# Distance attention: scores in 32x64 parts, weighted values in 128x32 parts, one element deeper

## What is computed

```python
x = x + _L0_xattn_ref(_layernorm(x), ctx, ctx, W_q, W_k, W_v, W_o, query_pos, key_pos, mask)
# in it, b = 32 elements, 16 heads:
scores = jnp.einsum('bhqd,bhkd->bhqk', Q, K) * scale
dist = (query_pos[:, :, None] - key_pos[:, None, :]).astype(scores.dtype)
scores = scores + -_slopes(NUM_HEADS)[None, :, None, None] * dist[:, None, :, :]
scores = jnp.where(mask[:, None, :, :] == 0, -jnp.inf, scores)
m = jnp.max(scores, axis=-1, keepdims=True)
e = jnp.exp(scores - m)
attn = e / (1.0 + jnp.sum(e, axis=-1, keepdims=True))
out = jnp.einsum('bhqk,bhkd->bhqd', attn, V)       # then @ W_o.T
```

## Time and profile before

| | us |
|---|---|
| median of 3 runs (753.58 to 753.89) | 753.7 |
| span of the profiled execution | 751.1 |
| PE busy in it | 662.8 |
| DVE busy | 485.5 |
| ACT busy | 365.0 |
| POOL busy | 310.1 |

### The profile page before, as it was taken

One profiled execution on the slowest core, in us unless ns is written; L12 is line 12 of the kernel. 1 busy time (PEld: TensorE's weight loads), 2 busy tenths in 40 slices (PEclk: granted clock), 3 DMA queues, 4 the chain that ended last, 5 costly groups with the idle time before them and its releaser, 6 DMA issues.

```text
span 751.1 us, 16917 instructions
## 1 busy us (share of the span) xinstructions
PE 662.8 (88%) x6115; PEld 500.4 (67%) x6115; DVE 485.5 (65%) x1367; ACT 365.0 (49%) x992; POOL 310.1 (41%) x458
## 2 busy tenths in 40 slices
PE   4899999999999989985994799988999776999990
PEld 3677878787777778753443586667877673777760
DVE  2686777677768669885488873558888875333330
ACT  1454545545555479874395653436566431222320
POOL 1235455646453179850000031136556513556541
PEclk9999999999999999996997699999999986999995
DMA  8723222322220000019200434538001022243434
GB/s 265 245 62 79 64 78 65 78 65 75 68 72 14 1 3 4 3 44 332 103 0 1 156 125 177 217 125 367 2 3 65 3 99 53 47 69 58 68 40 70
DMA packets 31697, 65.08 MB, mean 87 GB/s; under 512 B 5792, under 2 KB 21792, under 8 KB 29312
## 3 DMA queue, kind: packets, MB, share of 16 engines
q1 hardware_dynamic: 26016, 55.73, 22.8%
q0 software_dynamic: 4688, 7.18, 6.0%
q10 hardware_dynamic: 912, 1.10, 0.5%
HBM read 57.67 MB, written 7.37 MB: 87 GB/s over the span
## 4 chain that ended last, share of the span: by engine, by line
PE 64%; DVE 21%; ACT 5%; issue 4%; DMA 2%; SPq 2%; POOL 1%; DVEq 0%; ACTq 0%; POOLq 0%
PE psum L2627 7%; PE psum L474 6%; PE psum L482 6%; PE psum L496 5%; PE psum L2637 4%; PE psum L521 4%; PE psum L507 4%; PE psum L1482 3%; PE psum L1459 3%; PE psum L837 2%; DVE ff_peak L1500 2%; PE psum L846 2%; PE psum L829 2%; PE psum L877 2%; DMA wn<-in_w_down 2%
## 5 line engine op out<-in xcount | busy, mean ns | idle before, releaser
L415 ACT ACTIVATE prob<-s_sb,negm 128x257 f32<-128x257 f32 x128 | 66.2, 517 | 94.5 <-DVE negm L640 94.5
L782 POOL TENSOR_SCALAR bias<-dist,cst 128x257 f32<-128x257 f32 x128 | 59.8, 486 | 99.5 <-DVE dist L627 89.6
L636 DVE CUSTOM_DVE_ANT_0 s_sb<-psum,bias 128x257 f32<-128x257 f32 x128 | 49.4, 423 | 51.7 <-PE psum L496 48.4
L474 PE MATMUL psum<-ctxT,shared 128*128 128x257 f32 x256 | 62.6, 388 | 2.7 <-DMA msk<-in_mask 2.7
L482 PE MATMUL psum<-shared,ctxT 128*128 128x256 f32 x256 | 60.4, 379 | 0.0
L2627 PE MATMUL psum<-ex_w,shared 128*128 x184 | 58.3, 460 | 0.6 <-ACT shared L2520 0.6
L1721 POOL TENSOR_TENSOR wn<-wn,cst 128x1 f32<-128x1 f32 x8 | 4.7, 589 | 120.4 <-DVE wn L1848 120.4
L474 PEld LDWEIGHTS psum<-ctxT,shared 128*128 128x128 f32 x256 | 47.2, 195 | 9.0 <-issue 3.4
L482 PEld LDWEIGHTS psum<-shared,ctxT 128*128 128x128 f32 x256 | 48.4, 189 | 6.8
L496 PE MATMUL psum<-kT,qbd 64*128 64x257 f32 x256 | 48.4, 429 | 3.0 <-DVE mx L636 2.9
L2627 PEld LDWEIGHTS psum<-ex_w,shared 128*128 128x128 f32 x184 | 33.1, 190 | 15.4 <-issue 0.8
(11 more groups left out here) (359 smaller groups left out, 1655.9 us busy)
## 6 DMA issues: line engine op xcount, KB each, us to landing
ctxT<-in_ctx_T SPq DMA_DIRECT2D x32, 257.0 KB
ex_w<-in_w SPq DMA_DIRECT2D x1, 5632.0 KB, 17.5
kpos<-in_kpos SPq DMA_DIRECT2D x32, 128.5 KB
msk<-in_mask SPq DMA_DIRECT2D x32, 128.5 KB
near_turned<-in_ctx_T_tiles SPq DMA_DIRECT2D x4, 1028.0 KB
ff_used_up<-in_ctx_T_tiles SPq DMA_DIRECT2D x4, 1028.0 KB
near_rows<-in_ctx_tiles SPq DMA_DIRECT2D x4, 1024.0 KB, 8.0
ff_used_up<-in_ctx_tiles SPq DMA_DIRECT2D x4, 1024.0 KB, 7.3
```

What stands on the lines that cost most here:

```text
L415: nc.scalar.activation(prob[n % 2][:, g, :], s_sb[n % 2][:, g, :], ACT.Exp, bias=negm[:, b, g:g + 1], accum_out=esum[t % 2][:, b, g:g + 1]) \
L474: ins = nc.tensor.matmul(kv[m][:, 0:SK], w["xa_k"][:, k, P * m:P * m + P], ctxT[n % BT][:, k, :], start=(k == 0), stop=(k == KT - 1))
L636: nc.vector.tensor_tensor_reduce(s_sb[n % 2][:, g, :], sc[g % 2][:, 0:SK], bias[n % 2][:, g, :], 1.0, float("-inf"), ALU.add, ALU.max, mx[ ...
L782: nc.gpsimd.tensor_scalar(bias[n % 2][:, g, :], dist[n % 2][:], c.slope[:, g:g + 1], 1.0, ALU.mult, ALU.mult).then_inc(bias_ready, 1)
```

## The change

- Scores: eight matmuls of 32x64 parts per element in place of four of 64x128. Row part g takes 32 features, column part m has 64 outputs, each of the four groups has a bank of its own. qbd has two heads where it had four. The banks of the turned probabilities are now two of the scores' banks.
- Which heads belong together changes: the constants for slopes and selection (sel, two, two_quarter) follow.
- Weighted values: 16 matmuls of 128x32 parts with 64 columns in place of 8 of 128x64 with 128 columns; a whole tile of results fits into bank oo, and own_heads_of picks once per tile, in two steps.
- spread(t): the same work in 128x32 parts.
- Distances: two VectorE operations in place of three, with the factor FAR in the slopes taken out again in the bias.
- The lists of all engines are put in a new order: TensorE issues scores(n), weighted(n-2), keys(n+1), turn_p(n-1), values(n+1); VectorE and ScalarE lists follow.

```diff
-        qbd = [sb(f"qbd{i}", [P, KT, BT, 4, SQ]) for i in range(2)]
-        sc, pt, kv, oo, misc = bank[0:2], bank[2:4], bank[4:6], bank[6], bank[7]
+        qbd = [sb(f"qbd{i}", [P, KT, BT, 2, SQ]) for i in range(2)]
+        sc, pt, kv, oo, misc = bank[0:4], bank[0:2], bank[4:6], bank[6], bank[7]
...
+        def turned_at(t):
+            return BT * t + (2 if t == 0 else 0)
...
+            for n in range(N + 1):
+                t = n // BT
                 exps(n - 1, 2)
+                exps(n - 1, 3)
+                if n + 1 < N:
+                    keys(n + 1, 0)
+                    keys(n + 1, 1)
+                if n >= N - 1:
+                    ratio.act(act, n - N - 2)
+                if t + 1 < NT and n == turned_at(t):
                     xT_copy(t + 1)
+                exps(n, 0)
+                if n >= 1:
+                    copy_turned(n - 1)
+                exps(n, 1)
+                if n + 1 < N:
+                    values(n + 1)
...
+            def scores(n):
                 t, b = n // BT, n % BT
+                pe.wait_ge(k_done[0], n + 1)
+                pe.wait_ge(k_done[1], n + 1)
+                pe.wait_ge(qbd_ready, t + 1)
+                at_least(pe, s_done, 4 * n)
+                at_least(pe, pt_done[0], n - 1)
+                at_least(pe, pt_done[1], n - 1)
+                for g in range(NG):
+                    rows = slice(SQ * g, SQ * g + SQ)
+                    for m in range(KT):
+                        ins = nc.tensor.matmul(sc[g][64 * m:64 * m + 64, 0:SK],
+                                               qbd[t % 2][rows, m, b, :, :].rearrange("p h q -> p (h q)"),
+                                               kT[n % 2][rows, m, :], start=True, stop=True)
+                    ins.then_inc(s_full, 1)
 
             def turn_p(n):
                 for j in range(2):
                     pe.wait_ge(p_ready, 4 * n + 2 * j + 2)
                     at_least(pe, pt_done[j], n)
+                    if n + 1 < N:
+                        pe.wait_ge(s_done, 4 * (n + 1) + j + 1)
...
-                if n % 2 == 0:
-                    at_least(pe, keys_read, n // 2)
-                for gp in range(KT):
+                if n % BT == 0:
+                    at_least(pe, keys_read, n // BT)
+                for m in range(KT):
+                    at = P * (n % BT) + 64 * m
                     for i in range(2):
-                        for half in range(2):
-                            g, at = 2 * gp + half, D * (n % 2) + P * gp
-                            ins = nc.tensor.matmul(oo[64 * half:64 * half + 64, at:at + P],
-                                                   v[n % BT][:, i, 64 * g:64 * g + 64], pT[n % 2][:, g, i, :],
-                                                   start=(n % 2 == 0 and gp == 0 and i == 0), stop=True,
+                        for g in range(NG):
+                            own = slice(SQ * g, SQ * g + SQ)
+                            ins = nc.tensor.matmul(oo[own, at:at + 64],
+                                                   v[n % BT][:, i, P * m + SQ * g:P * m + SQ * g + SQ],
+                                                   pT[n % 2][:, g, i, 64 * m:64 * m + 64],
+                                                   start=(n % BT == 0 and m == 0 and i == 0), stop=True,
...
+            for n in range(N + 2):
                 t, b = n // BT, n % BT
                 if n < N:
+                    scores(n)
+                if n >= 2:
                     weighted(n - 2)
                 if b == 2 and t > 0:
                     spread(t - 1)
+                if n + 1 < N:
+                    pe.wait_ge(ctx_loaded[(n + 1) % BT], 48 * ((n + 1) // BT + 1))
+                    keys(n + 1, 0)
+                    keys(n + 1, 1)
+                if t + 1 < NT and n == turned_at(t):
+                    turn_x(t + 1)
...
+                if 0 <= n - 1 < N:
+                    turn_p(n - 1)
+                if n + 1 < N:
+                    values(n + 1)
+                if t + 1 < NT and n == turned_at(t):
+                    queries(t + 1)
+                if b == 3 and t > 0:
+                    output(t - 1)
+            spread(NT - 1)
...
-                st.done(nc.vector.tensor_scalar(dist[n % 2][:], kpos[b][:], qposf[:, n:n + 1], None, ALU.subtract))
                 st.link(dve, nc.vector.tensor_scalar(shut[:], msk[b][:], 0.0, -BIG, ALU.is_equal, ALU.mult))
-                nc.vector.scalar_tensor_tensor(dist[n % 2][:], shut[:], BIG, dist[n % 2][:], ALU.mult, ALU.add) \
-                    .then_inc(dist_ready, 1)
+                nc.vector.scalar_tensor_tensor(dist[n % 2][:], kpos[b][:], qposf[:, n:n + 1], shut[:], ALU.subtract,
+                                               ALU.add).then_inc(dist_ready, 1)
...
+            def own_heads_of(t):
+                dve.wait_ge(pv_done, BT * (t + 1))
                 at_least(dve, oT_ready, t)
+                mine = o_keys[:].rearrange("p b j q -> p (b j) q")
+                src = oo[:].rearrange("p (n h q) -> p n h q", n=BT * KT, h=2)
+                st.link(dve, nc.vector.tensor_scalar(mine, src[:, :, 0, :], c.two[:, 0:1], None, ALU.mult))
+                nc.vector.scalar_tensor_tensor(mine, src[:, :, 1, :], c.two[:, 1:2], mine, ALU.mult, ALU.add) \
+                    .then_inc(keys_read, 1)
...
+            for n in range(N + 2):
                 t, b = n // BT, n % BT
+                if n < N:
+                    rows_max(n)
+                if n + 1 < N:
+                    distances(n + 1)
+                if n >= 1 and t + 1 < NT and n - 1 == turned_at(t):
+                    spread_queries(t + 1)
+                if 0 <= n - 1 < N:
+                    copy_turned(n - 1)
+                if n in (0, 1):
+                    (norm_stats, norm)[n](1)
+                if b in (2, 3) and t + 2 < NT:
+                    (norm_stats, norm)[b - 2](t + 2)
+                if b == 0 and t > 0:
+                    denominators(t - 1)
+                if b == 1 and t > 0:
+                    own_heads_of(t - 1)
+                if b == 2 and t > 0:
+                    combine(t - 1)
+                if b == 3 and t > 0:
+                    add_output(t - 1)
+                if 1 <= n < 4:
+                    scales(n - 1)
...
-                    nc.gpsimd.tensor_scalar(bias[n % 2][:, g, :], dist[n % 2][:], c.slope[:, g:g + 1], 1.0,
+                    nc.gpsimd.tensor_scalar(bias[n % 2][:, g, :], dist[n % 2][:], c.slope[:, g:g + 1], 1.0 / FAR,
                                             ALU.mult, ALU.mult).then_inc(bias_ready, 1)
```

More of the change, by code:

```diff
@@ L42 @@
 BIG = 3e38
+FAR = 2.0 ** 16
 LN_EPS = 1e-5
@@ L238, in __init__ @@
         self.ones = cst[:, C_ONES:C_ONES + SQ]
-        self.sel = cst[:, C_SEL:C_SEL + 64]
+        self.sel = cst[:, C_SEL:C_SEL + 64].rearrange("p (m n) -> p m n", m=KT)
+        self.two = cst[:, C_TWO:C_TWO + 2]
+        self.two_quarter = cst[:, C_TWOQ:C_TWOQ + 2]
         self.pair = cst[:, C_PAIR:C_PAIR + 2]
@@ new lines, in values, with copy_turned @@
+            def values(n):
+                act.wait_ge(v_full, n + 1)
+                at_least(act, pv_done, n - BT + 1)
+                nc.scalar.copy(v[n % BT][:], kv[0][:].rearrange("p (k n) -> p k n", k=2)).then_inc(v_done, 1)
+            def copy_turned(n):
+                act.wait_ge(pt_full, 2 * n + 2)
+                at_least(act, pv_done, n - 1)
+                nc.scalar.copy(pT[n % 2][:, 2:4, :, :], pt[1][:].rearrange("p (g i n) -> p g i n", g=2, i=2)) \
+                    .then_inc(pt_done[1], 1)
@@ new lines, in _ @@
+            xT_copy(0)
+            keys(0, 0)
+            keys(0, 1)
+            values(0)
+            act.wait_ge(misc_full, uses["vl", 0])
+            nc.scalar.copy(v_last[:], misc[:, 0:KT * NB].rearrange("p (k n) -> p k n", k=KT)).then_inc(misc_done, 1)
+            for n in range(N + 1):
+                t = n // BT
+                exps(n - 1, 2)
+                exps(n - 1, 3)
+                if n + 1 < N:
[4 more added lines that the diff above has]
+                if t + 1 < NT and n == turned_at(t):
+                    xT_copy(t + 1)
+                exps(n, 0)
[4 more added lines that the diff above has]
+                    values(n + 1)
@@ L531, in spread @@
                 for i, src in enumerate((last_own[t % 2], rden_own)):
[L532 to L536, removed]
+                    for m in range(KT):
+                        at = D * i + P * m
+                        for g in range(NG):
+                            ins = nc.tensor.matmul(misc[SQ * g:SQ * g + SQ, at:at + P], c.sel[:, m, :],
+                                                   src[:, g, :, :].rearrange("p b q -> p (b q)"),
+                                                   start=(i == 0 and m == 0), stop=True, skip_group_check=True)
                 ins.then_inc(misc_full, 1)
@@ L644, in spread_queries @@
                 at_least(dve, s_full, 4 * BT * (t - 1))
```

(32 more changed lines are left out.)

97 lines of the change are left out of this document (11 added, 86 removed).

## The result

| | us |
|---|---|
| changed kernel, median (714.49 to 715.59) | 714.8 |
| before, same chip (752.82 to 753.89) | 753.6 |
| ratio, 95% interval | 0.9495 (0.9475 to 0.9515) |
| span of the profiled execution | 712.7 (before 751.1) |

A forecast was written before the change was run, and what follows sets the result against it. TensorE's instruction list was taken as the bound. Gains of 8.5 us in the opening, 32.1 from scores(5) to scores(31) and 0 after sum to 40.6: 753.7 - 40.6 = 713 us, range 707 to 727.

The forecast's parts named there:

- The bound: Edited stage: TensorE's instruction list sets the period, 30.23 us per tile of four elements before, 25.6 after.
- Scores: Per element, 32x64 parts: all eight run at once, 0.63 us for all four banks, before 0.63 + 0.68 or more.
- Weighted values: Per element, 128x32 parts: four run at once and short matmuls keep up, 0.62 us, before 1.02.
- Rival A: Weighted values: short matmuls don't hide their weight loads, 1.02 us instead of 0.62, +12 us, 725 in all; chance 0.13.
- Transposes: Turning the probabilities, per element: 0.86 us, not 1.02, as the new order saves a shape change there.
- Do the others keep up?: Other engines within a tile: VectorE 17.8 us of 25.6, ScalarE 15.4, GpSimd 16.1; all waits costed at nothing.
- T + 5.95 of 6.33: T is an element's first scores; VectorE finishes merged own heads at T + 5.0 + 0.95, needed by 5.7 + 0.63.
- The opening: Stretch up to scores(5): VectorE's chain behind the weights' landing sets the pace; 8.5 us gained, between 4 and 10.
- The hand-over: From scores(31) to the next stage's steady steps: 12.9 us before, about 12.5 after; gain taken as 0, between -3 and +3.
- rival B: Opening or hand-over gives back gain, through VectorE's waits or ratio work queued ahead on ScalarE: +5 to 7, 719; chance 0.15.
- The later stages: From the hand-over to the span's end: not edited, no gain forecast (0).
- From span to time: Profiled span 751.1 us against the runs' median 753.7: the 2.6 more taken as all outside the span.

The follow-up runs named there:

- the run in halves: Changed kernel with the scores issued in two halves around the weighted values, as before the change: 731.0 us, 16.2 more than the changed kernel.
- the step moved: Changed kernel with ScalarE's second early ratio attention step issued after the last copy of turned probabilities: 713.6 us; repeated, 714.2 beside the changed kernel's 716.7.

## Why the prediction was right, step by step

- **The bound.** TensorE's list, before and after. Right: no gap in a tile, 25.81 us for 25.6.
- **Scores.** 0.63 forecast, 0.62 measured; full concurrency of eight parts, shown by the run in halves.
- **Weighted values.** 0.62 forecast, 0.58 measured. Rival A (1.02) didn't come about. The rule of a least distance of 25 ns between starts, of the Trainium skill ("TensorE: Matmul & The Clock Gate", "Wait — 56ns, not 53.3ns?"), would have put 32 starts at 0.80. The piece of 0.58 is 18 ns each with the change of shape in it, so the measurement decides against that rule for neighbours in different parts.
- **Transposes.** 0.86 forecast, 0.87 measured. But the shape change that I had given to the transposes has to be paid by whatever comes first after the tiled work, now the keys: 1.94, not 1.74. I had put 0.1 for all that; the term was short by 0.10 per element. The 0.04 won on the weighted values takes back part of it; 5.74 against 5.7 per element is left, most of the 0.2 per tile.
- **Do the others keep up?** Right that nothing stalls, and the date of the merged own heads, rated "met" at T + 5.95 of 6.33, was read nearly right: 0.38 of slack by that sum, 0.45 in the trace. What failed, without touching the number, is what I made of it: I named the copy of the values as the tightest at 0.2. It ends 0.62 us after the values (131.74 behind 131.12), which is 0.58 ahead of the keys where no spread stands between, the same distance that the own heads have. And I didn't see that the own heads' date is what the VectorE edit buys. VectorE is at 18.88 per tile, not 17.8; some operations that the edit leaves alone took longer than before (last_own up to 0.50 for 0.28, rden_own 0.97 for 0.78), and why stays open.
- **The opening.** 8.5 forecast, 8.2 measured: the size was luck. The forecast let VectorE's chain behind the weights' landing set the date both before and after. Before, the scales account for 2 us; after, TensorE's list sets it, busy for 29.18 of 30.13 us, and VectorE's chain ends within 1.1 us of it.
- **The hand-over.** Put at 0 between -3 and +3; it lost 2.5. I had summed it by prices and overlooked what the step of the ratio attention holds at its end, a norm that waits for GpSimd, ahead of the last copy. That is rival B as it was written (ratio work queues ahead on ACT, its sign 15.37 us against the 13.5 named), at half its price. With the step moved the stretch takes 12.34 us (213.82 to 226.16), near the 12.5 of the sum.
- **The later stages.** 1.8 us less without an edit. The ratio attention's steps keep their distances (L837 at 280.00 before and L856 at 243.46 after, and the last L904 at 333.54 and L923 at 297.00: 36.54 both times); what is left comes behind them. It isn't shown to be the change's: the changed kernel's two traces differ there by 4.4 us. Of the 38.4 us between the two spans the marks show 36.5.
- **From span to time.** I put all of the 2.6 us between the span of 751.1 and the median outside the span. Every execution on record shows 1.7 to 1.9 there (753.59 beside 751.8, for one); the rest was a profiled execution faster than the median. The forecast is the median less the gain, so it isn't touched.

## What to carry to other kernels

Price a list of an engine by the distances between its pieces, not by busy time, and charge each change of the array's shape to the piece behind it: two kinds of work in one shape belong side by side. Narrow parts pay only while neighbours in the list name different ones. And where an engine isn't the bound, look not at its share but for its dates: merging steps gives one step a date that several small ones hadn't, and the same work a little further on in the list costs next to nothing.

## What the runs showed of the hardware that I had not expected

- Matmuls named part by part: 36 ns each for 64 columns, neither the 13 of four parts at once nor the 53 of one at a time. Open why.
- A wait of 4.5 us on TensorE was followed by 2.75 us at clock 0.50; with the moved step no wait there was over 1.4 us, and the clock stayed at 1.00.
- A later stage's granted clock differed between two traces of the very same kernel (0.85 and 0.78 over about 80 us), and with it TensorE's busy time by 4.4 us, enough to hide a gain of 3 us.
